# Hybrid attention and expert kernel on one core: the first two batches' channel attention in the opening, from raw rows; the second block's routing later

## What is computed

```python
x = x + attn_a(layernorm(x))            # channel attention
x = x + ffn(layernorm(x))               # 8 experts, scored per token
x = x + attn_b(layernorm(x))            # token attention
x = x + ffn(layernorm(x))

def attn_a(x):                          # x: (4, 512, 128), already layer-normed
    xn = x * rsqrt(mean(x * x) + 1e-6) * norm_weight
    q, k, v = heads(xn @ w_qkv.T)       # 8 heads of 16 channels, tokens last
    q, k = q / |q|, k / |k|             # norms over the 512 tokens
    attn = softmax((q * exp(temperature)) @ k.T)     # 16 x 16 per head
    return (attn @ v) @ w_out.T

def ffn(h):
    probs = softmax(h @ router_w.T)
    k = argmax(gelu(h @ actor_w1.T + b1) @ actor_w2.T + b2) + 1
    scores = where(rank(probs) < k, probs, 0)
    return sum over 8 experts of scores[e] * down_e(silu(gate_e(h)) * up_e(h))
```

## Time and profile before

| | us |
|---|---|
| median of 3 executions | 488.22 |
| lowest, highest | 487.97, 489.9 |
| the profiled execution, its own time | 489.73 |
| its span | 487.9 |
| PE busy in the span | 476.1 (98%) |
| POOL, DVE, ACT busy | 312.4, 303.0, 266.2 |

### The profile page before, as it was taken

How to read it: one execution, slowest core, us unless ns; L and a number is a source line. 1 busy time by engine, 2 the same in 40 slices (tenths; PEclk the granted TensorE clock), 3 DMA queues, 4 the chain that set the end, 5 groups by cost and what they waited for, 6 DMA issues and landing times.

```text
span 487.9 us, 6499 instructions
## 1 busy us (share of the span) xinstructions
PE 476.1 (98%) x2039; PEld 342.7 (70%) x2039; DVE 303.0 (62%) x718; ACT 266.2 (55%) x484; POOL 312.4 (64%) x326
## 2 busy tenths in 40 slices
PE   8899899999999999999999999999999999999997
PEld 7777666677676666666676766677676777778886
DVE  3656342646487768499836884359754565666563
ACT  3395636646724693348742649235772456456551
POOL 5355789336948576486463466467675586778774
PEclk9999899999999999999999999999999999999999
DMA  7700000000000000000000000000000000000000
GB/s 240 247 0 2 0 1 0 1 1 1 1 0 2 1 0 1 1 1 1 0 1 0 1 2 0 1 1 5 19 0 2 0 23 1 0 1 10 15 0 22
DMA packets 7933, 7.36 MB, mean 15 GB/s; under 512 B 732, under 2 KB 7772, under 8 KB 7900
## 3 DMA queue, kind: packets, MB, share of 16 engines
q1 hardware_dynamic: 7900, 6.96, 4.4%
HBM read 5.91 MB, written 1.05 MB: 14 GB/s over the span
## 4 chain that ended last, share of the span: by engine, by line
PE 83%; ACT 2%; DVE 1%; POOL 1%; issue 0%; ACTq 0%; DVEq 0%; POOLq 0%
PE bank L1313 21%; PE bank L1128 17%; PE bank L1130 17%; PE bank L1129 17%; PE bank L1351 3%; PE bank L1249 1%; PE bank L1343 1%; PE bank L1151 1%; PE bank L1363 1%; PE bank L1321 1%; PE bank L1257 1%; PE bank L1291 1%; ACT L778 1%; PE bank L1239 0%; PE bank L1219 0%
## 5 line engine op out<-in xcount | busy, mean ns | idle before, releaser
L647 POOL TENSOR_TENSOR t<-t,sl 128x512 f32<-128x512 f32 x105 | 148.6, 1421 | 80.9 <-DVE t L1069 61.7
L778 ACT ACTIVATE sl<-bank 128x512 f32<-128x512 f32 x168 | 99.2, 596 | 126.3 <-PE bank L1130 114.5
L1313 PE MATMUL bank<-t,WD 128*128 128x512 f32 x256 | 126.0, 592 | 0.0
L1069 DVE TENSOR_TENSOR t<-bank,sbc 128x512 f32<-128x512 f32 x105 | 72.3, 689 | 72.2 <-PE bank L1130 70.5
L1128 PE MATMUL bank<-xhF,WGh 128*128 128x512 f32 x167 | 89.8, 538 | 1.0 <-ACT sl L778 0.9
L647 POOL TENSOR_TENSOR t<-t,sbc 128x512 f32<-128x512 f32 x63 | 79.4, 1288 | 0.2
L1069 DVE TENSOR_TENSOR t<-bank,sl 128x512 f32<-128x512 f32 x63 | 42.9, 686 | 55.8 <-ACT sl L778 30.0
L1128 PE MATMUL bank<-xhF,WUh 128*128 128x512 f32 x168 | 66.8, 397 | 1.1 <-DVE t L1069 1.1
L1130 PE MATMUL bank<-xhF,WUl 128*128 128x512 f32 x168 | 66.3, 395 | 0.0
L1129 PE MATMUL bank<-xlF,WUh 128*128 128x512 f32 x168 | 66.3, 394 | 0.0
L1130 PE MATMUL bank<-xhF,WGl 128*128 128x512 f32 x167 | 66.2, 397 | 0.0
(11 more groups left out here) (210 smaller groups left out, 722.9 us busy)
## 6 DMA issues: line engine op xcount, KB each, us to landing
stage<-in_gate SPq DMA_DIRECT2D x7, 192.0 KB, 5.7
stage<-in_up SPq DMA_DIRECT2D x7, 192.0 KB, 5.7
WD<-in_down SPq DMA_DIRECT2D x7, 192.0 KB, 5.7
X<-in_x SPq DMA_DIRECT2D x4, 256.0 KB, 5.4
out<-X SPq DMA_DIRECT2D x3, 256.0 KB, 2.3
raw<-in_small SPq DMA_DIRECT2D x1, 384.0 KB, 4.2
out<-X SPq DMA_DIRECT2D x2, 128.0 KB, 1.9
raw<-in_small SPq DMA_DIRECT2D x1, 192.0 KB, 2.7
```

Of the source, the lines that this page charges most:

```text
L647: pool.tensor_tensor(t2[k % NT2][:, :], t2[k % NT2][:, :], by[:, :], ALU.mult).then_inc(a_done, 1)
L778: act.activation(sl[k % NSL][:, :], bank[k % 2][:, :], ACT.Silu).then_inc(silu_done, 1)
L1069: dve.tensor_tensor(t2[k % NT2][:, :], bank[2 + k % 2][:, :], by[:, :], ALU.mult).then_inc(t2_done, 1)
L1313: r = pe.matmul(OACC[:, :], WD[:, c, :], t2[k % NT2][:, :], start=(c == 0), stop=(c == CH - 1 or k == TAIL[0] - 1))
```

## The change

- **Opening.** For batches 0 and 1 the rows aren't normed first. Batch 0 and 1 are transposed as they were loaded. The mean is taken out of the q, k, v and weights side instead: `cenw` = (identity - 1/128) scaled by `norm_weight` is multiplied with all 384 weight columns on PE (`wn`) and copied back to `raw` by ACT. The Gram matrix is raw rows times rows divided by the variance (`rinv`, a DVE reciprocal, no power), and the power -0.5 per token is applied when DVE adds `y` to x (one scalar_tensor_tensor a tile). For batch 0 the v rows are computed up front (`vT`, 512 columns), so `am2` of batch 0 is gone.
- Batch 1's remaining steps move from slots 3 to 15 into the opening; `ss`, `rs`, `qn` get second buffers and its sums of squares a step of their own (`asq`). A Silu on one column (`silu`) brings the silu set in ahead of slot 0.
- Warming multiplies zeros that DVE sets first, not the identity; 22 matmuls in place of 35.
- `x` of batch 1 and `cols` are loaded ahead of the first expert weights. The head mask is made by three POOL instructions in place of 24.
- Block 1's layer norm and routing stand in slots 4 to 24, where they stood in 16 to 32; batch 2's channel attention starts at slot 9.

```diff
-PRELUDE = [("stats", "A", 0), ("rstd", "A", 0), ("warm", 0), ("xn", "A", 0), ("ag", 0), ("xT", "A", 0), ("ar", 0), ("wph", 0), ("wph", 1),
...
+PRELUDE = [("warm", 0), ("xT", "A", 0), ("warm", 1), ("stats", "A", 0), ("rstd", "A", 0), ("wn", 0), ("xn", "A", 0), ("ag", 0),
+           ("stats", "A", 1), ("rstd", "A", 1), ("xn", "A", 1), ("ar", 0), ("ag", 1), ("asq", 0), ("asim", 0), ("ass", 0), ("apow", 0),
+           ("wph", 0), ("wpl", 0), ("ar", 1), ("vT", 0), ("wph", 1), ("asq", 1), ("ascale", 0), ("ass", 1), ("apow", 1), ("asT", 0),
+           ("asim", 1), ("amax", 0), ("aexp", 0), ("warm", 2), ("ascale", 1), ("asT", 1), ("awo", 0), ("amax", 1), ("am", 0), ("aexp", 1),
+           ("wpl", 1), ("warm", 3), ("awo", 1), ("silu", 0), ("y", 0), ("am", 1), ("xT", "A", 1), ("wv", 0), ("swh", 0), ("am2", 1),
+           ("warm", 4), ("stats", "F", 0), ("rstd", "F", 0), ("wp", 3), ("xn", "F", 0), ("xT", "F", 0), ("xl", "F", 0), ("wp", 4),
+           ("y", 1), ("swl", 0)]
-WARM = (12, 2, 4, 7, 10)
+WARM = (6, 5, 3, 2, 6)
-A1_STEPS = [(2, "asim"), (3, "ass"), (3, "apow"), (4, "ascale"), (7, "asT"), (7, "amax"), (8, "aexp"), (9, "awo"),
-            (11, "am"), (12, "am2"), (14, "y")]
-F1_STEPS = [(0, "stats"), (0, "rstd"), (0, "xn"), (3, "xT"), (4, "xl"), (6, "route"), (7, "inner", 0), (8, "rt"), (9, "rcmp"), (9, "rexp"),
+F1_STEPS = [(5, "stats"), (6, "rstd"), (8, "xn"), (10, "xT"), (11, "xl"), (13, "route"), (14, "inner", 0), (15, "rt"), (16, "rcmp"), (16, "rexp"),
...
-A_STARTS = (7, 24)
+A_STARTS = (9, 24)
...
             sp.dma_start(X[:, 0:NT, :], xv[:, 0]).then_inc(x_loaded[0], 16)
+            sp.dma_start(cols[:, :], cols_d).then_inc(cols_loaded, 16)
             sp.dma_start(raw[:, 0:C_OUT], small_d[:, 0:C_OUT]).then_inc(qkv_loaded, 16)
-            sp.dma_start(cols[:, :], cols_d).then_inc(qkv_loaded, 16)
+            sp.dma_start(X[:, NT:2 * NT, :], xv[:, 1]).then_inc(x_loaded[1], 16)
...
+                if kind == "wn":
+                    act.wait_ge(wn_full, 1)
+                    act.activation(raw[:, 0:C_OUT], bank[2][:, 0:C_OUT], ACT.Copy).then_inc(wn_ready, 1)
+                if kind == "vT":
+                    act.wait_ge(vT_full, 1)
+                    act.activation(YT[:, :], bank[0][:, :], ACT.Copy).then_inc(vT_ready, 1)
+                if kind == "silu":
+                    act.activation(junk[:, :], cols[:, 5:6], ACT.Silu)
...
+            dve.tensor_scalar(cenw[:, :], ident[:, :], 1.0 / D, None, ALU.subtract).then_inc(ci_ready, 1)
...
+                    if seq < 2:
+                        rinv = rinvs[seq]
+                        dve.wait_ge(stats_ready, seq + 1)
+                        chain(dve.tensor_scalar(rinv[:, :], mv[:, :, 1], 1.0 + RMS_EPS, RMS_EPS * LN_EPS, ALU.mult, ALU.add))
+                        chain(dve.reciprocal(rinv[:, :], rinv[:, :]))
...
-                            r = dve.tensor_tensor(X[:, i, :], bank[i][:, 0:P], X[:, i, :], ALU.add)
+                            r = dve.scalar_tensor_tensor(X[:, i, :], bank[i][:, 0:P], rstds[0][:, i:i + 1], X[:, i, :], ALU.mult, ALU.add)
...
-                        pe.matmul(OACC[:, 0:P], ident[:, :], ident[:, :], start=True, stop=True)
+                        pe.matmul(OACC[:, 0:P], sl[0][:, 0:P], sl[0][:, 0:P], start=True, stop=True)
...
+                if kind == "wn":
+                    pe.wait_ge(cenw_ready, 1)
+                    pe.wait_ge(qkv_loaded, 16)
+                    pe.matmul(bank[2][:, 0:C_OUT], cenw[:, :], raw[:, 0:C_OUT], start=True, stop=True).then_inc(wn_full, 1)
+                if kind == "vT":
+                    pe.wait_ge(wn_ready, 1)
+                    wait_free(pe, turn_of["xT", "A", 0])
+                    pe.matmul(bank[0][:, :], raw[:, C_QKV + 256:C_QKV + 384], xaT[0][:, :], start=True, stop=True).then_inc(vT_full, 1)
...
-                        r = pe.matmul(m[:, 0:P], xn[:, i, :], xn[:, i, :], start=(i == 0), stop=(i == NT - 1))
+                        r = pe.matmul(m[:, 0:P], xn[:, i, :] if b > 1 else X[:, NT * b + i, :], xn[:, i, :], start=(i == 0), stop=(i == NT - 1))
...
-                        r = pe.matmul(to, xaT[b % 2][:, a], mixw[:, :], start=True, stop=True)
+                        r = pe.matmul(to, xaT[b % 2][:, a] if b else YT[:, a], mixw[:, :] if b else mix[:, :], start=True, stop=True)
```

More of the change, by code:

```diff
@@ L150, in needs @@
     if kind == "xT" and s[1] == "A":
-        return [("y", b - 2), ("ag", b)]
-    if kind == "am2" and b == 0:
+        return [("y", b - 2), ("ag", b)] if b > 1 else []
+    if kind == "am2" and b == 1:
         return [("wv", 0)]
@@ L378, in build @@
         ones = sb("ones", [P, 1])
+        junk = sb("junk", [P, 1])
+        cenw = sb("cenw", [P, P])
+        rinvs = [sb(f"rinv{i}", [P, NT]) for i in range(2)]
         hmask = sb("hmask", [P, P])
@@ L566, in _ @@
             pool.memset(nhalf[:, :], -0.5).then_inc(consts_ready, 1)
-            head_mask(range(H // 2))
+            own = hmask[:, :].rearrange("p (e d) -> p e d", d=DH)
+            chain(pool.memset(hmask[:, :], 0.0))
+            chain(pool.affine_select(out=own, in_=own, compare_op=ALU.is_ge, fill=NEG, base=0,
+                                     pattern=[[-DH, H], [0, DH]], channel_multiplier=1))
+            pool.affine_select(out=own, in_=own, compare_op=ALU.is_ge, fill=NEG, base=DH - 1,
+                               pattern=[[DH, H], [0, DH]], channel_multiplier=-1).then_inc(consts_ready, 1)
             for s in steps:
@@ L1177, in _ @@
                       .then_inc(m_full[t % 3], 1)
+                if kind == "asq":
+                    b = s[1]
+                    wait_free(pe, turn_of["ar", b])
+                    for j in range(2):
+                        r = pe.matmul(bank[1 + 2 * b][:, P + j:P + j + 1], qsq[:, 1 - j, :], ones[:, :], start=True, stop=True)
+                    r.then_inc(squares_full, 1)
                 if kind == "asim":
```

127 lines of the change are left out of this document (67 added, 60 removed).

## The result

| | before | changed | ratio, 95% interval |
|---|---|---|---|
| median, us | 488.13 (9 runs, 487.97 to 489.9) | 490.76 (9 runs, 490.36 to 491.05) | 1.0038 [1.0025, 1.0051] |
| profiled execution, us | 489.73 | 490.82 | |
| its span, us | 487.9 | 488.8 | |

The forecast was 483.0 with a range of 480.5 to 487.0. The changed kernel takes 490.8: slower by 2.6 us or 0.4%, a small difference, but clear of the noise and not in the direction of the forecast. So some 7.8 us of the forecast are missing, and the profile has to say where.

What follows compares the result with a forecast made beforehand. PE was taken as the bound, busy 476.1 of 487.9 us. Slots: 7.2 us that could go less 1.95 given back, net -5.2; opening 0; set on the median 488.22, this gave 483.0, range 480.5 to 487.0.

Steps and rivals of the forecast that it cites:

- Batch 1's work off the slots, 2.1: In the slots: PE loses batch 1's similarity, squares, y, asT, am and am2, 2.1 us in sum.
- The gaps of 1.91 and 0.41 go: PE gaps before 70 us: 1.91 goes with batch 1's table loads, 0.41 as block 1's rows come earlier.
- Slots 5 and 7 wait, 0.6 and 0.8: Given back: slot 5's gate product waits 0.6 for silu; 0.8 of the small gaps stays, behind block 1's statistics.
- the 0.3 and 0.25 for the routing and the Gram matrix: Given back: block 0's routing waits 0.3 for SWl; ACT evicts the Gram matrix 0.25 late before ar.
- none over 0.5 at slots 12 to 18: Sign expected in the new profile: no PE gap over 0.5 us at slots 12 to 18.
- The slow clock of 1.7: Behind the 1.91 gap, PE's granted clock of 0.51 for 3.50 us loses some 1.7 us, which goes.
- The sum is a difference, so I set it on the median: Final step: the net -5.2 us was set on the median 488.22, not the profiled execution's 489.73, giving 483.0.
- The opening, 0: Before slot 0: more work in the same time, no gain; slot 0 at 23.4, with 0.5 either way.
- The silu load: Opening: a 1.28 us load on ACT between batch 1's wo and mix, ending by 19, just covered.
- The clock's fall in the opening: Rival, 14%: PE idles 1.4 us between wv and batch 1's am2, the clock falls; price 1.7, time 485.0.
- From 70 us to the end there is none: PE timeline reading: no gap after 70 us, so nothing later shortens except by taking work from PE.
- The rival of the moved gap: Rival, 15%: POOL delivers batch 2's norm late, slot 14 waits and the clock falls; 3.6 us, time 486.6.

Runs made afterwards that it cites:

- e3: The kernel before the change, with all 35 warming matmuls on zeros in place of the identity; 488.32 us, 1.0001 of before.
- e2: The changed kernel with one weight piece (ScalarE copy and GpSimd subtraction) moved behind block 0's first rows in the opening; 490.3 us, 1.0032 of before.
- e1: The changed kernel with batch 1's token attention allowed to start at slot 52 in place of 48; 488.27 us, 0.9989 of before.
- e5: e1 with block 1's rank and maximum put into slot 16 ahead of its exponentials; 486.84 us, 0.9959 of before.
- e7: e1 with A_STARTS back from (9, 24) to (7, 24), so block 2's routing comes earlier; 486.35 us, 0.9952 of before.
- e6: e1 with block 1's last routing steps (act, actk, sx, sbc) eight slots later, at slots 29 to 32; 486.78 us, 0.9966 of before.

## Why the forecast was wrong

By its own steps:

- **Batch 1's work off the slots, 2.1: right in kind, a little small.** The work between slot 0 and 167 fell by 2.8 (against e3, whose clock was full).
- **The gaps of 1.91 and 0.41 go: right.** Neither stands in the changed kernel.
- **Slots 5 and 7 wait, 0.6 and 0.8: right.** Measured 0.70 before slot 5's gate product; 0.21 and 0.53 before two up products, 0.74. Together with the 0.3 and 0.25 for the routing and the Gram matrix, for which no gap shows, the forecast gave back 1.95; measured 1.44. Its sign "none over 0.5 at slots 12 to 18" fails at the end of the stretch, with the 1.19 behind slot 17.
- **The slow clock of 1.7: mis-set.** It was read from an execution of 489.73 us and taken off a median of 488.22, which was that of executions without it. "The sum is a difference, so I set it on the median" is the sentence at fault: a difference that contains a loss of only some executions may be set on those alone. Against executions at a clock of 1.00 the forecast's own terms give -3.5, some 484.7, still 6 us under the result.
- **The opening, 0: right in total, by two errors that cancel.** It had slot 0 at 23.4. The profiled execution has 24.0, with a fall of the clock that cost 1.0; the six others with this opening and no fall have 23.0 to 24.1. The silu load was hidden, as the row of 1.28 said. Missed was the tile that takes 1023 ns beside GpSimd, 0.8 (e2); the chain ahead of it was up to 1.1 faster than priced (block 0's statistics at 17.3 to 18.4, where the forecast had 18.4). That these two about balance is luck. The clock's fall in the opening, a rival with 14% at 1.7 us, came in the profiled execution, but from 15 to 18 us and so before the place that it named, the gap ahead of `am2`; that gap was 0.75, and 1.25 in e1 with the clock at 1.00.
- **"From 70 us to the end there is none", and nothing would come: the step that failed.** First, the reading was wrong: there was a gap of 0.90 at 301 (harmless, it is in both kernels). Second and above all, the forecast costed the steps that the change names and left the rest as it was, while the planner lays the slots up to 82 anew: a term put at nothing without a look at the plan. There 5.47 of gaps arose between 149 and 219 us, and 1.19 at 63. These 6.7, with 0.4 for the start of slot 0, less 0.7 of work and 0.5 of small gaps that came better than priced, make the 5.8 between the -3.5 above and the +2.3 measured on the spans. e1 (one entry, -2.5), e5 (rank first, -1.4), e7 (batch 2's start, -1.9) and e6 (-1.5) show the gaps to be matters of placement. The rival of the moved gap had the right idea, but one gap, at slot 14, where there is none.

What stays open: how the gaps between 149 and 163 us divide between the missing down products and the late routing of block 2 (e7 moves both at once), why the opening's first 7 us differ from one execution to the next, and what decides, after the same gap, whether the clock falls.

## What to carry to other kernels

Where a planner orders the work, compare the whole plan of both kernels slot by slot before costing anything; every step that moved is part of the change, and the stretch with no gap before is where new ones can open. When a profiled execution and the median differ by more than the spread of a group of runs, find the term in the profile that makes the difference before using it. And after moving something early, try the neighbours' start slots one by one: single entries were worth 1.9 to 2.7 us here, as much as the change itself. Read an opening by its parts, or from several executions: here its total differed by 1.2 us with nothing changed.
